# Inverse denominators copied out by DMA instead of by matmuls, residual sums one batch earlier, and the loads of the joining stage in another order

## The reference, cut to what matters

```python
x = x + attn(layernorm(x))          # causal softmax over 16 heads, ctx @ W_O
xf = layernorm(x).reshape(-1, 256)
logits = xf @ Wr / temp
topw, topi = jax.lax.top_k(logits, 2)
topw = jax.nn.softmax(topw, axis=-1)
for e in range(8):
    a, g = jnp.split(xf @ W1[e] + b1[e], 2, axis=-1)
    y = a * jax.nn.silu(g) @ W2[e] + b2[e]
    out = out + y * we              # we: this token's weight for e, or 0
x = x + out
```

## Time and profile before

| | |
|---|---|
| median of 3 runs | 1150.02 us (1148.51 to 1151.36) |
| the profiled execution's own time | 1161.29 us |
| its span | 1159.5 us |
| mean granted TensorE clock | 0.931 |
| PE, DVE, ACT, POOL busy | 1044.3, 762.8, 503.1, 411.0 us |

### The profile page before, as it was taken

How to read it: one execution, slowest core, us unless ns; L and a number is a source line. 1 busy time by engine, 2 the same in 40 slices (tenths; PEclk the granted TensorE clock), 3 DMA queues, 4 the chain that set the end, 5 groups by cost and what they waited for, 6 DMA issues and landing times. The chain is left out here.

```text
span 1159.5 us, 19495 instructions
## 1 busy us (share of the span) xinstructions
PE 1044.3 (90%) x5364; PEld 549.1 (47%) x5365; DVE 762.8 (66%) x2270; ACT 503.1 (43%) x1060; POOL 411.0 (35%) x781
## 2 busy tenths in 40 slices
PE   5998999999999999999877730899999999999995
PEld 2443333333333333335546630466666666666663
DVE  3776999999999898896435432455555555555552
ACT  2553377777777777775343330122222222222221
POOL 5566233333333333342263345022222222222222
PEclk9997599999999999999797755899999999999998
DMA  2869766665555444414238573122222222222222
GB/s 88 261 229 264 140 129 131 133 131 129 120 120 121 85 84 85 84 41 123 92 102 299 193 234 110 35 45 46 47 45 45 45 45 45 45 45 45 45 45 27
DMA packets 102395, 121.22 MB, mean 105 GB/s; under 512 B 26352, under 2 KB 81776, under 8 KB 102320
## 3 DMA queue, kind: packets, MB, share of 16 engines
q1 hardware_dynamic: 89024, 102.55, 35.1%
q0 software_dynamic: 13296, 17.77, 9.0%
HBM read 70.27 MB, written 49.63 MB: 103 GB/s over the span
## 5 line engine op out<-in xcount | busy, mean ns | idle before, releaser
L740 ACT ACTIVATE b_prob<-bank 128x512 f32<-128x512 f32 (+3 forms) x768 | 312.8, 507 | 91.2 <-PE bank L784 90.7
L766 PE MATMUL bank<-b_k_st,b_q_st 96*128 96x512 bf16 (+3 forms) x768 | 255.6, 346 | 5.5 <-DVE b_neg_max L694 1.7
L694 DVE CUSTOM_DVE_ANT_0 bank<-bank,b_mask_max 128x256 f32<-128x256 f32 (+3 forms) x512 | 241.2, 507 | 24.5 <-PE bank L766 24.4
L652 POOL TENSOR_SCALAR_AFFINE_SELECT b_prob<-b_prob 128x128 f32<-128x128 f32 x512 | 145.9, 294 | 307.1 <-ACT b_prob L740 302.4
L784 PE MATMUL bank<-b_q_st,b_k_st 99*128 99x512 bf16 (+3 forms) x768 | 245.5, 335 | 3.2 <-ACT b_prob L740 1.1
L1644 POOL DMA_INDIRECT out_dram<-e_y,e_token x71 | 110.7, 1560 | 325.0 <-DVE e_y L1698 313.7
L697 DVE TENSOR_REDUCE b_neg_max<-bank 128x1 f32<-128x512 f32 x256 | 175.6, 686 | 13.6 <-PE bank L766 11.1
L805 PE MATMUL bank<-b_prob,b_v_aug 128*32 128x512 f32 (+3 forms) x1536 | 145.8, 498 | 0.0
L1768 PE MATMUL e_y_ps<-w_sb,e_hiddenT 128*128 x568 | 134.4, 379 | 1.8 <-ACT e_hiddenT L1721 1.8
L1751 PE MATMUL e_g_ps<-w_sb,e_rowsT 128*128 x284 | 135.4, 599 | 0.4 <-issue 0.4
L1751 PE MATMUL e_a_ps<-w_sb,e_rowsT 128*128 x284 | 133.4, 592 | 0.0
(11 more groups left out here) (172 smaller groups left out, 1007.6 us busy)
## 6 DMA issues: line engine op xcount, KB each, us to landing
w_sb<-in_L_ffn_W SPq DMA_DIRECT2D x12, 1024.0 KB
e_rows<-slot_rows SPq DMA_DIRECT2D x72, 129.0 KB, 2.0
ctx_cols<-b_ctx_out SPq DMA_DIRECT2D x16, 512.0 KB
q_parts<-a_part_q SPq DMA_DIRECT2D x8, 768.0 KB, 4.0
k_parts<-a_part_k SPq DMA_DIRECT2D x8, 768.0 KB, 4.8
b_q_st<-q_parts SPq DMA_DIRECT2D x16, 384.0 KB, 4.8
b_k_st<-k_parts SPq DMA_DIRECT2D x16, 384.0 KB, 8.1
a_x<-in_L_attn_x SPq DMA_DIRECT2D x8, 512.0 KB, 5.0
```

What stands on the lines that cost most here:

```text
L652: nc.gpsimd.affine_select(out=prob[n % NP][:, 0:P], in_=prob[n % NP][:, 0:P], compare_op=ALU.is_ge, fill=0.0, base=0, pattern=[[1, P]], ch ...
L694: nc.vector.tensor_tensor_reduce(scores, scores, mask_max[:, HALF - width:HALF], -1.0, -MASKED, ALU.add, ALU.min, to).then_inc(max_done, 1)
L740: nc.scalar.activation(prob[n % NP][:, 0:width], prob_ps[n % NS][:, 0:width], ACT.Exp, scale=SCALE).then_inc(prob_ok, 1)
L766: nc.tensor.matmul(out[:, 0:width], q_st[g % RING][0:STACK, h, i * P:(i + 1) * P], k_st[g % RING][0:STACK, h, half * HALF:half * HALF + wi ...
```

## The change

It has four parts.
1. The inverse sums are stored to a new DRAM tensor `ctx_invs` (`store_inverse`) and loaded again with each row repeated for 16 partitions (`load_scale`, two DMAs of 512 KB each per batch) into `c_scale`. The spread matmuls, the matrix on POOL and their bank bookkeeping go. `invert` for batches 0 and 1 moves into attention on DVE (`INVERT_AT`).
2. DVE's order: `scale_heads(1)` stands ahead of `first_normalise`; `residual` and `moments` of batch b + 1 stand ahead of `choose(b)`; `scale_heads(3)` between `choose(1)` and `slots(1)`.
3. PE's slots: projections of batch 0 at 5 to 11, of batch 1 at 39 to 45; `turn` of batch 0 from slot 20; project(2) ahead of turn(1), project(3) behind counts(1).
4. SP's order is new, the bias loads go to its end behind the second scatter of batch 1, and batch 1 gets a second row buffer of its own. POOL scatters batch 0's second rows ahead of its wait for the end of attention.

```diff
+PROJECT_0 = (5, 7, 9, 11)
+TURN_0 = (20, 22, 25, 28)
+ROUTER_0 = (22, 25, 28, 30)
+COUNT_0 = 37
+PROJECT_1 = (39, 41, 43, 45)
+INVERT_AT = (9 * UNITS + PER_HALF, 13 * UNITS + PER_HALF)
+ROOT_AT = TOTAL - 12
...
+    def store_inverse(self, sp, b):
...
+        sp.dma_start(self.dram["inv"][b * HEADS:(b + 1) * HEADS, :].rearrange("h (t n) -> (h t) n", n=P),
+                     self.inv_den[:]).then_inc(self.inv_den_st, 16)
+
+    def load_scale(self, sp, b):
+
+        sp.wait_ge(self.inv_den_st, 16 * (b + 1))
+        if b:
+            sp.wait_ge(self.heads_ok, b * SCALES)
+        for c in range(DC):
+            of = self.dram["inv"][b * HEADS + c * P // HD:b * HEADS + (c + 1) * P // HD, :]
+            sp.dma_start(self.scale[:, c, :], of.unsqueeze(1).to_broadcast([P // HD, HD, SEQ])).then_inc(
+                self.scale_in_ok, 16)
+
...
+        sp.wait_ge(self.v_aug_ok, NQUAD)
+        sp.dma_start(self.wo[:], w_o.rearrange("(c p) n -> p c n", p=P)).then_inc(self.small_in, 16)
         sp.wait_ge(self.prob_sc_ok, PER_QUAD * (NQUAD - 2))
+        self.load_scale(sp, 0)
         self.load_x(sp, 1)
...
     def sync_second(self, sp):
 
-        sp.wait_ge(self.proj_ok, PAIRS)
+        self.load_scale(sp, 1)
         self.load_heads(sp, 1)
         self.store_x2(sp, 0)
+        self.store_inverse(sp, 2)
+        self.load_x(sp, 2)
+
+    def sync_third(self, sp):
+
+        self.load_scale(sp, 2)
+        self.load_heads(sp, 2)
+        self.store_x2(sp, 1)
...
+        self.load_den(sp, 3)
+        self.load_heads(sp, 3)
+        self.store_inverse(sp, 3)
+        self.load_scale(sp, 3)
+        self.load_x(sp, 3)
+        self.store_x2(sp, 2)
+        for f in range(1, FC):
+            load_w2(f)
...
+        self.store_x2(sp, 3)
+
+        sp.wait_ge(self.second_in_slot, 16 * BT * 2)
+        for e in range(EXPERTS):
+            for n in range(2):
+                sp.dma_start(self.bias[n][:, e, :], b_dram[n][e:e + 1, :].to_broadcast(
+                    [P, b_dram[n].shape[1]])).then_inc(self.loaded, 16)
...
-        invert(1)
+        self.invert(dve, 2)
         dve.wait_ge(self.small_in, 48)
         then(nc.vector.reciprocal(self.inv_temp[:], self.temp_in[:]))
+        scale_heads(1)
         first_normalise()
         choose(0)
         slots(0)
-        scale_heads(1)
+        residual(1)
+        moments(1)
+        scale_heads(2)
         for b in range(1, BATCH):
-            residual(b)
-            moments(b)
+            shift(b)
+            if b == 1:
+                self.invert(dve, 3)
             if b + 1 < BATCH:
-                invert(b + 1)
-            shift(b)
-            if b + 1 < BATCH:
-                scale_heads(b + 1)
+                residual(b + 1)
+                moments(b + 1)
             choose(b)
+            if b == 1:
+                scale_heads(3)
             slots(b)
         tables()
...
+        for t in range(PAIRS):
+            self.project(pe, 2, t)
         for b in range(1, BATCH):
...
             self.counts(pe, b)
-            if b + 1 < BATCH:
-                for t in range(PAIRS // 2, PAIRS):
-                    self.project(pe, b + 1, t)
+            if b == 1:
+                for t in range(PAIRS):
+                    self.project(pe, 3, t)
```

More of the change, by code:

```diff
@@ L685, in _ @@
             g = unit // UNITS
+            if unit in INVERT_AT:
+                route.invert(dve, INVERT_AT.index(unit))
             for n in range(unit * QUAD, (unit + 1) * QUAD):
@@ L852 @@
 PAIRS = BT // 2
-SPREADS = DC * SEQ // CHUNK
+SCALES = DC * SEQ // CHUNK
 BIG = 3.0e38
[L857 to L865, removed]
+PROJECT_0 = (5, 7, 9, 11)
[3 more added lines that the diff above has]
+PROJECT_1 = (39, 41, 43, 45)
+NARROW = [(kind, b, t) for kind, b in (("project", 0), ("turn", 0), ("project", 1)) for t in range(PAIRS)]
+INVERT_AT = (9 * UNITS + PER_HALF, 13 * UNITS + PER_HALF)
+ROOT_AT = TOTAL - 12
 POWER_AT = TOTAL - 6
@@ L1019, in store_x2, with denominators @@
                      self.x2[b % 2][:]).then_inc(self.x2_st[b % 2], 16)
+    def denominators(self, sp, b):
+        for p in range(2):
+            sp.wait_ge(self.ctx_st[p], 32 * 2 * (b + 1))
+        self.load_den(sp, b)
     def sync_first(self, sp):
         _, w_o, w_r, temp, _, _ = self.sources
[L1024 to L1027, removed]
         sp.wait_ge(self.prob_sc_ok, PER_QUAD * (NQUAD - 3))
@@ L1193, in wide @@
             return ap.unsqueeze(2).to_broadcast([P, ap.shape[1], n])
-        def invert(b):
-            dve.wait_ge(self.den_in_ok[b % 2], 16 * (b // 2 + 1))
-            if b:
-                dve.wait_ge(self.spread_ps_ok, b * SPREADS)
-            nc.vector.reciprocal(self.inv_den[:], self.den_in[b % 2][:]).then_inc(self.inv_den_ok, 1)
         def scale_heads(b):
             dve.wait_ge(self.heads_in_ok, 16 * (b + 1))
-            for k in range(SPREADS):
-                half = self.heads[:, k % DC, k // DC * CHUNK:(k // DC + 1) * CHUNK]
-                dve.wait_ge(self.spread_ps_ok, b * SPREADS + k + 1)
-                nc.vector.tensor_tensor(half, half, self.spread_bank(b, k)[:], ALU.mult).then_inc(self.heads_ok, 1)
+            dve.wait_ge(self.scale_in_ok, 16 * DC * (b + 1))
+            for k in range(SCALES):
+                half = slice(k // DC * CHUNK, (k // DC + 1) * CHUNK)
+                nc.vector.tensor_tensor(self.heads[:, k % DC, half], self.heads[:, k % DC, half],
+                                        self.scale[:, k % DC, half], ALU.mult).then_inc(self.heads_ok, 1)
         def residual(b):
@@ L1353, in vector @@
         dve.wait_ge(self.const_ok, 6)
-        invert(0)
         scale_heads(0)
@@ L1521, in between @@
             self.counts(pe, 0)
-        if slot in SPREAD_1:
-            self.spread_out(pe, 1, SPREAD_1.index(slot))
         if slot in PROJECT_1:
@@ L1817, in build @@
             route = Route(nc, life, early, freed, after, bias, banks, dram, x, w_o, w_r, temp, (b1, b2), w2, w2_sb,
-                          loaded, out)
+                          loaded, second_row, out)
             w2_sb += [after(f"w2_sb{f}", [P, EXPERTS, D]) for f in range(FC_EARLY, FC)]
```

158 lines of the change are left out of this document (61 added, 97 removed).

## The result

The changed kernel takes 1157.49 us (median of 6 runs, 1154.74 to 1158.62), the kernel before 1150.06 beside it: ratio 1.0062, 95% interval 1.0051 to 1.0074. It is slower by 0.6%, where 1127.0 was forecast. The profiled execution of the changed kernel took 1156.59 of its own.

What follows compares the result with a forecast made beforehand. The loop from one batch's row numbers to the next bounds the joining stage, POOL's scattering next. +2.2 (tail), -3.6 (first batch), -26.6 (POOL), +5 (stops) gave -23.0: 1150.0 becomes 1127.0 us, range 1119 to 1138.

Steps and rivals of the forecast that it cites:

- tail, E' against E: End of the stage's tail (last products), changed kernel against before: 602.1 for 599.86 us, +2.2, waiting for POOL's cuts.
- from the tail to S: From the tail's end to the first scatter of batch 1: 25.4 us where before took 29.0, -3.6.
- from S to X: From batch 1's first scatter towards the experts' first rows: POOL no longer idles, 88.5 us becomes 61.9, -26.6.
- stops: ACT or PE standing still in two full-DMA stretches of 5 to 6 us each: 5 charged, bounds 0 and 12.
- the unknown price: Rate of the repeated load, which no row showed: taken as that of the heads; other bound twice that time.
- The rival that said so (0.28): Repeated loads go at half rate, since their source's outermost dimension is 8: tail ends 4.5 us later, 1131.5 us; chance 0.28.
- just in time: Under the half-rate case, batch 3's inverses arrive near 18.5 us behind the tail's end, just in time.
- the forecast's own wait of 3 us: In the tail, PE waits 3 us at slot 5 for batch 0's scaled heads before it may project.
- The reciprocals: Two in attention on DVE, 0.95 us each, where PE hardly waits for that engine: no cost.
- the sums hidden in the wait for the logits: Next batch's residual and moments on DVE, 6.3 us, hidden while it waits for logits in each loop round.
- 1.5 us in hand at a batch: Batches 2 and 3: row numbers come near 44.2 and 65.1 us behind the tail, POOL is ready at 45.8 and 66.5.
- Slower: Repeated load on the path twice in the tail; above 15 us per 1 MB the kernel is slower; chance 0.04.

Runs made afterwards that it cites:

- one row, 16: Changed kernel, but each repeated load takes one row of inverses over all 128 partitions, not 8 rows 16 times each; heads scaled by wrong numbers: 1139.15 us.
- 4 blocks: Changed kernel, but the scale loads read 128 rows of x as 4 blocks of 32 (outermost dimension 4): 1184.24 us beside 1162.4 for before.
- the kernel before, once more: The kernel before, unaltered, profiled again beside its timed runs: 1150.69 us, ratio 1.0006; its profiled execution took 1149.81.
- second repair: Changed kernel with denominators stored twice, four of batch 0's first scatters behind POOL's cuts, batch 1's heads scaled behind batch 0's normalisation: 1137.39 us; 1159.61 where before takes 1164.05.
- 128 rows apart: Changed kernel, but the scale loads read 128 different rows of x of the same size; heads scaled by wrong numbers: 1138.12 us, ratio 0.9892.

## Why the prediction was wrong

**The bound and the mechanism of the gain were right.** Behind the first scatter of batch 1 POOL takes 62.5 us without a gap (forecast 61.9), and the experts start as close behind it as before. What came of each term, from the traces of an ordinary execution of before (E 598.3, 29.6 us to S, 86.0 us to X), of one row, 16, where the load is fast, and of the changed kernel:

| term, us | forecast | one row, 16 | changed kernel |
|---|---|---|---|
| tail, E' against E | +2.2 | +4.4 | +14.5 |
| from the tail to S | -3.6 | -0.7 | +7.4 |
| from S to X | -26.6 | -15.4 | -15.4 |
| stops | +5 | 0 | 0 |
| sum | -23.0 | -11.7 | +6.5 |

**Failed first: the unknown price, "The nearest are the heads, 1 MB in 4 KB rows, and I took that".** The load runs on half the DMA engines. The rival that said so (0.28) had the right cause and too small a size: 4.5 us later at E', 1131.5. By one row, 16 against the changed kernel, the first scaling is 6.0 us later (540.46 for 534.49), the second 11.8, E' 10.0 and the first scatter 18.2 (649.83 for 631.65), and the kernel 18 us slower. Three things make the difference to that rival. 1 MB at 163 GB/s is 6.4 us, 3.3 more than at 332 and not 2.7. While x of batch 1 is beside it only 196 GB/s move, at a full DMA share, where one row, 16 has 306 to 386; and what is queued behind it (batch 1's heads) is as late. And the last load, forecast as "just in time", came 10.0 us late (2.25 with one row), which alone is 8.1 of the 18.2. The rival's own sum also slipped: 2.8 and 2.7 behind 556.0 is 561.5 and not 560.5. The Trainium skill ("DMA: Bandwidth & Descriptors", Why a DMA increments its semaphore by 16 and not by 1) gives 8 engines for this load, and by that rule 4 for 4 blocks; the shares of 0.52, 0.53 and 0.26 agree.

**Failed second: -26.6 for the loop, "88.5 becomes 61.9".** The 88.5 was read from an execution 11.3 us above the median, and I took the 11.3 to be spread evenly, off both sides of the sum. It lay in this very loop: in an ordinary execution the same stretch is 77.7 (627.91 to 705.64, the end of the last scatter of the kernel before, once more). So only 15.2 us were there to be had. This mis-sized term costs 11 of the forecast 23 us. That the rest then fits the loads at full rate (1138.1 and 1139.2, 11 to 12 us below before) is partly luck: the allowance of 5 that was not needed makes up for 5.1 us missing in the two terms above it.

**Those two terms, with a fast load.** The tail gains 2.2 us more than forecast, in which the first two projections stand at the low clock behind PE's wait for the scaled heads: 3.75 us for the first, not 1.89, and 2.65 for the second. It is 3.75 with the fast load (wait 3.23) as with the slow one (9.47), so the forecast's own wait of 3 us should have been charged with it. The step from the tail to S lacks 2.9 us: project(2) takes 8.68 and not 6.9, since PE waits 2.80 us for POOL's cuts just ahead of it and goes on at the low clock (7.14 once that wait is gone, 10.16 in the changed kernel), and DVE waits 2.25 us for the last load. The reciprocals and the sums hidden in the wait for the logits came as forecast; moving these sums back costs 11.8.

**The allowance of 5 for stops** fits no chip. It was 0 on the two where before takes 1150. On the one where before takes 1164 it was 22 for the second repair (1159.6 less 1137.4) and 23 for the changed kernel, of which before itself has 12 to 14. The new order is hit harder; by the forecast POOL has 1.5 us in hand at a batch, and the stops are longer. The rule of the Trainium skill ("Runtime: NRT & Kernel Launch", Instruction fetch mechanics), by which fetches are mostly hidden, would fit the first two chips; no row names the fetch on the others, and what stops ACT and DVE there stays open.

**Slower came by the mechanism of that rival** (the load on the path, 0.04), helped by a gain only half as large. The rival had the load on the path twice and needed 15 us for each; it is there three times, and the slow rate costs 6.0, 5.8 and 8.1 us, of which 1.8 come back in the tail.

## What to carry to other kernels

Before a DMA is priced by its bytes, look at the outermost dimension on both sides: with 8 here only half of the 16 engines worked, with 4 a quarter, and the loads behind it in the queue were late too. Storing a row twice bought back 14.5 us, and still left the load slower than 128 rows apart. Before a term is read from a profile, set its own time against the median: if the profiled execution is long, ask where, for the excess may be the very wait that is to be removed. A wait of a few us that a forecast puts ahead of PE has a second price, the low clock behind it (1.9 us on the first projection here). A gain that is measured on one chip may shrink on another (1.2% and 0.3% here), so compare with the old kernel on the same one.

## What the runs showed of the hardware

A load whose source has an outermost dimension of 8 keeps the 16 DMA engines busy for 0.53 of the time and moves about 163 GB/s; with 4 it is 0.26 and 104 GB/s. With 16 rows, each for 8 partitions, the engines are all busy and 224 GB/s move, where 128 rows apart have 326 in the same window.

The same kernel differs by 12 to 23 us between chips. On the slower ones ACT idles for 3.6 to 12.8 us in rows ahead of the last copies of a batch that name no releaser, and DVE for 6.0 to 8.8 us once, ahead of the logits of batch 3. The stops of ACT occur at a DMA share of 0.18 as at 1.1. The mean granted clock is 0.935 and 0.930 for before, and 0.931 and 0.923 for the second repair; PE idles more where the others stop. The first profile of before has such a stop too (6.45 us), beside timed runs of 1150; whether it ran on the same chip as these is not on record. The cause was not found.
